# Four-tap convolution in a Mamba input stage: one tap and the bias made by ScalarE from the projection's PSUM bank

## The reference, cut to what matters

```
xz = layernorm(hidden) @ in_proj_w              # 256 -> 1024
x, z = split(xz, 2)                             # 512 and 512 channels
xpad = pad(x, 3 zeros ahead of each sequence)
acc = sum over k in 0..3 of conv_w[:, k] * xpad[:, k:k + seqlen, :]
x = silu(acc + conv_b)
x_dbl = x @ x_proj_w                            # 64 for dt, 16 for B, 16 for C
dt = softplus(dt_low @ dt_proj_w + dt_bias)
u = dt * x                                      # "du"; silu(z) is used later on
```

## Time and profile before

| | |
|---|---|
| runs | 2545.29, 2545.34, 2553.23 us (median 2545.34) |
| profiled execution | 2548.63 us, span 2546.9 us |
| TensorE busy | 2258.4 us (89%) |
| VectorE busy | 1786.6 us (70%) |
| ScalarE busy | 1339.8 us (53%) |
| GpSimd busy | 1340.4 us (53%) |
| mean granted clock of TensorE | 0.948 of full |
| the stage | from 0 to some 230 us |

### The profile page before, as it was taken

One profiled execution on the slowest core, in us unless ns is written; L12 is line 12 of the kernel. 1 busy time (PEld: TensorE's weight loads), 2 busy tenths in 40 slices (PEclk: granted clock), 3 DMA queues, 4 the chain that ended last, 5 costly groups with the idle time before them and its releaser, 6 DMA issues. The chain is left out here.

```text
span 2546.9 us, 34973 instructions
## 1 busy us (share of the span) xinstructions
PE 2258.4 (89%) x11358; PEld 1329.1 (52%) x11359; DVE 1786.6 (70%) x2734; ACT 1339.8 (53%) x2581; POOL 1340.4 (53%) x1024
## 2 busy tenths in 40 slices
PE   8895888989988988599986699999998569999998
PEld 3342444544544545599973334444444336666666
DVE  6998999999999997655557899999993651111100
ACT  5777887787788786322224456666665311111110
POOL 1545999899899895377755312222222123334332
PEclk9997999999999999799997789999998779999999
DMA  5457245125125112644437612222200503333322
GB/s 165 150 186 260 102 131 194 37 77 185 42 77 180 50 50 85 190 71 72 72 60 165 144 33 34 34 42 42 34 3 4 199 25 83 66 71 70 74 50 25
DMA packets 149681, 231.36 MB, mean 91 GB/s; under 512 B 26257, under 2 KB 98769, under 8 KB 149394
## 3 DMA queue, kind: packets, MB, share of 16 engines
q1 hardware_dynamic: 120258, 190.44, 24.8%
q0 software_dynamic: 29280, 39.11, 9.5%
HBM read 152.43 MB, written 81.66 MB: 92 GB/s over the span
## 5 line engine op out<-in xcount | busy, mean ns | idle before, releaser
L1263 POOL TENSOR_TENSOR scan_hC<-scan_h,scan_c_all 128x1024 f32<-128x1024 f32 x256 | 612.5, 2416 | 65.0 <-DVE scan_h L1118 63.8
L1118 DVE TENSOR_TENSOR_SCAN scan_h<-scan_dA,banks 128x1024 f32<-128x1024 f32 x224 | 504.5, 2275 | 21.3 <-ACT scan_dA L1040 12.9
L893 PE MATMUL banks<-scan_hC,all_ident 128*128 128x512 f32 x1024 | 486.9, 600 | 26.4 <-DVE scan_xc L1125 26.4
L2346 ACT ACTIVATE attn_pt<-banks 128x1024 f32<-128x1024 f32 (+3 forms) x384 | 292.3, 810 | 183.1 <-PE banks L2293 180.2
L1033 ACT ACTIVATE scan_scaled<-mamba_duT,mamba_bT 128x128 f32<-128x128 f32 x1024 | 312.0, 388 | 20.5 <-PE banks L870 20.1
L2230 POOL TENSOR_SCALAR_AFFINE_SELECT attn_pt<-attn_pt 128x256 f32<-128x256 f32 x256 | 102.6, 407 | 376.7 <-ACT attn_pt L2346 375.0
L893 PEld LDWEIGHTS banks<-scan_hC,all_ident 128*128 128x128 f32 x1024 | 185.3, 191 | 179.3 <-issue 129.2
L3084 DVE TENSOR_TENSOR ffn_y<-banks,ffn_gates 128x512 f32<-128x512 f32 x32 | 22.1, 691 | 334.7 <-PE banks L2842 328.0
L3131 POOL DMA_INDIRECT out<-ffn_y,ffn_ids x64 | 105.3, 1645 | 270.5 <-DVE ffn_y L3084 260.8
L2368 DVE TENSOR_REDUCE attn_m_lo<-banks 128x1 f32<-128x512 f32 (+3 forms) x368 | 225.9, 657 | 26.3 <-PE banks L2249 20.0
L2249 PE MATMUL banks<-attn_K,attn_Q 96*128 96x512 bf16 (+3 forms) x768 | 230.9, 340 | 7.1 <-DVE attn_mask L2358 5.9
(11 more groups left out here) (354 smaller groups left out, 3873.5 us busy)
## 6 DMA issues: line engine op xcount, KB each, us to landing
scan_c_all<-scratch_bc SPq DMA_DIRECT2D x64, 512.0 KB, 5.8
ffn_w<-in_e_w SPq DMA_DIRECT2D x16, 1024.0 KB, 5.4
attn_Q<-scratch_q SPq DMA_DIRECT2D x96, 128.0 KB, 4.1
scratch_x<-front_xc SPq DMA_DIRECT2D x8, 1024.0 KB, 5.8
scratch_z<-front_zs SPq DMA_DIRECT2D x8, 1024.0 KB, 7.5
scan_xc<-scratch_x SPq DMA_DIRECT2D x16, 512.0 KB, 3.6
scan_zs<-scratch_z SPq DMA_DIRECT2D x16, 512.0 KB, 4.6
scratch_dt<-front_lw SPq DMA_DIRECT2D x7, 1024.0 KB, 4.1
```

The source lines that it names most:

```text
L893: mm = pe.matmul(PS[:, YB + i, :], ident[:, :], hC[:, u % NHC, i * BANK:(i + 1) * BANK], start=s == 0, stop=s == NST - 1, skip_group_check ...
L1118: dve.tensor_tensor_scan(h[:, u % NH, :], decay, drive, 0.0, ALU.mult, ALU.add).then_inc(scanned, 1)
L1263: pool.tensor_tensor(hC[:, u % NHC, :], h[:, u % NH, :], c_all[:, s, :], ALU.mult).then_inc(hC_done, 1)
L2346: act.activation(pt[:, at % 4, 2 * pair:2 * pair + 2, 0:width], PS[:, ST + 2 * pair:ST + 2 * pair + 2, 0:width], ACT.Exp, scale=HD ** -0.5 ...
```

## The change

ScalarE now does two things with each bank of x: first it makes `conv = taps[3] * bank + cbias` (an Identity activation with scale and bias read per partition), counted by a new semaphore `own_tap`; then it copies the bank into `xpad` as before. VectorE makes three operations where it made four: tap 0 is added to `conv` into the accumulator bank, tap 1 to the accumulator, tap 2 to the accumulator into `conv`. ScalarE waits for the weights' loads before its first step, and the wait for the SiLU of the chunk before, which frees `conv`, moves from VectorE to ScalarE.

```
+        DTAPS = NTAP - 1
+        own_tap = n.sem("own_tap")
 def copy_x(q, m):
     act.wait_ge(in_psum, 2 * MT * q + m + 1)
     h = q % HB
     if q >= HB:
-        act.wait_ge(conv_step, NTAP * (MT * (q - 1 if h == 0 else q - HB) + m + 1))
+        act.wait_ge(conv_step, DTAPS * (MT * (q - 1 if h == 0 else q - HB) + m + 1))
+    if q:
+        act.wait_ge(silu_x, MT * (q - 1) + m + 1)
+    act.activation(conv[:, m, :], PS[:, bank_of("x", q, m), :], ACT.Identity, scale=taps[:, m, DTAPS:NTAP],
+                   bias=cbias[:, m:m + 1]).then_inc(own_tap, 1)
     act.activation(xpad[:, m, NTAP - 1 + h * CH:NTAP - 1 + (h + 1) * CH], PS[:, bank_of("x", q, m), :],
                    ACT.Copy).then_inc(x_copied, 1)
 def silu_conv(q, m):
-    act.wait_ge(conv_step, NTAP * (MT * q + m + 1))
+    act.wait_ge(conv_step, DTAPS * (MT * q + m + 1))
...
 act.wait_ge(made, 4)
+loads.wait(act)
...
 def convolve(q, m):
     h = q % HB
     acc = PS[:, CBANK, :]
-    for tap in range(NTAP):
+    for tap in range(DTAPS):
         src = xpad[:, m, h * CH + tap:h * CH + tap + CH]
         if tap == 0:
+            dve.wait_ge(own_tap, MT * q + m + 1)
             dve.wait_ge(x_copied, MT * q + m + 1)
-            if q or m:
-                dve.wait_ge(conv_step, NTAP * (MT * q + m))
-            dve.tensor_scalar(acc, src, taps[:, m, 0:1], cbias[:, m:m + 1],
-                              ALU.mult, ALU.add).then_inc(conv_step, 1)
-        else:
-            dve.wait_ge(conv_step, NTAP * (MT * q + m) + tap)
-            if tap == NTAP - 1 and q:
-                dve.wait_ge(silu_x, MT * (q - 1) + m + 1)
-            dve.scalar_tensor_tensor(out=conv[:, m, :] if tap == NTAP - 1 else acc, in0=src,
-                                     scalar=taps[:, m, tap:tap + 1], in1=acc, op0=ALU.mult,
-                                     op1=ALU.add).then_inc(conv_step, 1)
+        if q or m or tap:
+            dve.wait_ge(conv_step, DTAPS * (MT * q + m) + tap)
+        dve.scalar_tensor_tensor(out=conv[:, m, :] if tap == DTAPS - 1 else acc, in0=src,
+                                 scalar=taps[:, m, tap:tap + 1], in1=conv[:, m, :] if tap == 0 else acc,
+                                 op0=ALU.mult, op1=ALU.add).then_inc(conv_step, 1)
```

## The result

The changed kernel takes 2553.05 us (median of 22 runs, 2550.76 to 2556.26). The kernel before takes 2548.38 (median of 22 runs, 2545.29 to 2553.23), 3.0 above the median of the three runs that the prediction started from. The medians are 4.7 us apart. The ratio of the runs is 1.0016, 95% interval 1.0009 to 1.0022: 4.1 us slower (2.3 to 5.6). That lies within the 0.3% that were called no change, but it is not zero, and the time is 1 us over the range.

What follows compares the result with a forecast made beforehand. VectorE and TensorE were taken as nearly tied, VectorE holding TensorE through ScalarE's copies. Terms + 0.7 + 0.7 + 1.3 - 0.8 - 1.8 gave + 0.1 us, so 2545.5 from a median of 2545.34; range 2540 to 2552.

Steps and rivals of the forecast that it cites:

- rival (b): Identity makes ScalarE load tables ahead of x_proj, 2 x 1.28 us a step: + 18, 2563 us; chance 0.04.
- step 0: First step: the tap ahead of the copy of x(0,3) makes TensorE 0.7 us later.
- the stall of dt(1): TensorE's wait for VectorE's `less` before chunk 1's dt projection, 5.86 us before, stays, near 6.5 us.
- Steady steps: From one x_proj to the next: 22.32 us for 22.53, a gain of 0.8 us over four steps.
- rival (a): VectorE's relief reaches the stage's end, TensorE runs without stalls: - 13.6, 2531.8 us; chance 0.08 in full.
- weak form: Rival (a) with the standard deviation half as late and taps near 0.6 us: - 5, 2540 us; chance 0.08.
- signs of being wrong: A `less` stall under 3 us, steps of 21.8, or the stage's last VectorE instruction moved over 4 us.
- the price of tap 0 within its bounds: VectorE's new tap 0, two SBUF inputs, result in PSUM: 756 ns taken, bounds 0.62 and 0.81 us.
- the tail: Stage's end: less VectorE backlog before the last SiLU turns + 2.0 us into + 0.15, a gain of 1.8.
- The stall of 0.55 us a step: TensorE, ready at 133.84, waits before x_proj for ScalarE's copy of x(5,1), behind its tap, until about 134.40.
- rival (c): Slightly slower: ScalarE taps of 1.0 us and a longer lower clock behind the stall: + 4 to + 6, 2550 us; chance 0.10.

Runs made afterwards that it cites:

- e7: Changed kernel with GpSimd's products dt and du cut to 8 of 512 columns: 2551.97 us, ratio 1.0012.
- e12: Changed kernel, but tap 0's second input is the accumulator bank in PSUM, not conv in SBUF: 2549.34 us, ratio 1.0006.
- e13: e12 with ScalarE's square root of the next group moved right behind the copy of x(q,0): 2540.72 us, ratio 0.9972.
- e2: Kernel before with VectorE's tap 3 left out and no new work on ScalarE: 2542.05 us, ratio 0.9976.
- e6: Changed kernel with the square root early and ScalarE's taps made from xpad behind the copies: 2542.71 us, ratio 0.9982.
- e9: Kernel before with the change for groups 2 and 3 alone, taps from xpad behind all copies, and the square root early: 2537.44 us, ratio 0.9965.
- e10: Kernel before with the change for groups 2 and 3 alone, taps from xpad behind all copies, square root not moved: 2549.69 us, ratio 1.0008.
- e5: Kernel before with only ScalarE's square root moved right behind the copy of x(q,0): 2541.08 us, ratio 0.9973.
- e8: Kernel before with GpSimd's products dt and du cut to 8 of 512 columns: 2544.79 us, ratio 0.9987.

## Why the prediction was wrong

**The median it started from**: of the 7.5 us between 2545.5 and 2553.05, 3.0 are the kernel before, whose 22 runs lie that much over the first three. 4.7 are the change, of which 0.1 was forecast. The range was missed by 1 us, and each of two errors is larger than that: this median, and the operand below.

**What was right.** The length of ScalarE's tap (0.77 forecast, 0.780), and that there are no further table loads (rival (b)). By the Trainium skill, "ScalarE: Activation LUTs", What ACT_TABLE_LOAD costs, the estimate was 0.80. TensorE 0.7 us late in step 0, once the later start is taken off; the square root of group 2 behind the taps; the stall of dt(1) at 6.34 us for "near 6.5". The square root's end lets VectorE's reciprocal begin, 66.44 for 65.26, and 0.7 of that is the start of the stage:

```profile
66.44 0.25 DVE L483 RECIPROCAL front_rstd<-front_rstd 128x16 f32<-128x16 f32 x1 [8.70 <-ACT front_rstd L347]
```

Steady steps of 22.32 were forecast; with all four of ScalarE's taps ahead of the copies they are 22.45 wherever VectorE is out of the way (e7, e12, e13). A dt(1) waiting over 3 us rules out rival (a), and e2 shows what its relief alone is worth: 6.1 us, the size of its weak form. Of the signs of being wrong one came: the stage's last VectorE instruction begins at 232.85 for 228.64, 4.2 us later.

**The step that failed: "VectorE's work in a step falls from 21.6 us ... to 18.3, so it has slack, and the price of tap 0 within its bounds costs nothing."** The price was outside the bounds: 0.985 us in the mean, up to 1.72 beside GpSimd. All the rows that bounded it have only one of their input tensors in SBUF. The Trainium skill, "GPSIMD Engine Reference", Key points, says that GpSimd shares its SBUF interfaces with VectorE and contends with its instructions that have two SBUF inputs: the rule that spoke against this change, and I hadn't weighed it. The traces agree: 0.985 us beside GpSimd at work, 0.761 with it quiet (e7), 0.753 with one input in PSUM (e12). The slack went into stretched operations, tap 0 and more still the short ones, whose price the sum of 18.3 had left as it was. So VectorE stayed 19.35 us busy of 20, where 17 were forecast, and with the long tap 0 it was late for the last SiLU of step 5. The operand's place is worth 2.1 us of the stage by e12 against the changed kernel: some 0.5 by x_proj(1) and dt(1) (GpSimd's rows come later too, and the transposes wait 1.65 us for them, 1.17 in e12 and 0.49 before), 0.2 of slow clock, 1.1 by the stall of 1.81 us, 0.3 in the tail. In the tail VectorE's softplus begins at 204.79, behind the split of B and C, though its Exp had ended at 204.0:

```profile
200.54 1.63 DVE L530 TENSOR_TENSOR front_bc_rest<-front_xd,mamba_bc_parts 32x512 f32<-32x512 f32 x1
202.21 1.38 DVE L532 CAST front_bc_mid<-front_bc_rest 32x512 bf16<-32x512 f32 x1
203.62 0.42 DVE L533 CAST mamba_bc_parts<-front_bc_rest 32x512 bf16<-32x512 f32 x1
...
204.79 1.23 DVE L512 TENSOR_SCALAR front_w<-front_u 128x2048 f32<-128x2048 f32 x1
```

**The stall of 0.55 us a step**, mis-sized: 0.68 measured, since x_proj starts 0.14 us after the copy's end and not 0.04. With a slow clock behind dt(1) that lasts a little longer (6.61 us for 6.10), and the rest of the tail, this is 1.3 us of the stage. It is what remains of rival (c), whose taps of 1.0 us did not come.

**The start**: 0.7 us of the 4.1 that the stage missed its forecast by (0.7 + 2.1 + 1.3) lie ahead of the first tap. Bank x(0,1) was read at 18.62 before and 19.32 after:

```profile
19.32 0.78 ACT L360 ACTIVATE front_conv<-banks,mamba_cbias,mamba_taps 128x512 f32<-128x512 f32 x1 [1.06 <-PE banks L284]
```

TensorE's instructions up to there are the same in both. The kernels with ScalarE's tap in this place read it between 18.36 and 20.03, those without any ScalarE tap between 18.41 and 18.79, and those with the tap elsewhere (e6, e9, e10) at 19.93, 19.48 and 18.65. Whether a part of it belongs to the change stays open.

**What the change could give.** With the square root and the operand out of the way (e13) the change is level with its counterpart (e5). So with the taps ahead of the copies nothing was to be gained even with tap 0 at the 0.75 us that I took. Taps behind the copies with a cheap tap 0 were not run, and what they would give stays open. By e12 the time would have been 2549.34 with that tap 0, in the range.

## What to carry to other kernels

An operation moved off an engine can change the ones that stay: count where each remaining operand lies, and what GpSimd does at that time, before you call the engine relieved. Taking work from the busiest engine pays only up to the next loop, so work out that engine's step first; here it was 22.45 us for 22.53. And look for the one instruction that stands behind others in a queue: moving a square root ahead of Exp and three copies was worth more than any division of the taps tried here.

## What the runs showed of the hardware

- A slowed engine doesn't show as idle, and relief of it need not show as idle time either (19.17 of 20 us in e12). Tap 0 takes 0.74 to 0.76 us alone, often 1.20 beside GpSimd and at most 1.72. VectorE's short casts stretch far more in proportion, 0.41 to 1.38 us for 32x512, and GpSimd's product `du` from 1316 to 1466 ns:

```profile
123.50 0.76 DVE L502 SCALAR_TENSOR_TENSOR banks<-front_xpad,mamba_taps,front_conv 128x512 f32<-128x512 f32 x1
...
125.97 1.20 DVE L502 SCALAR_TENSOR_TENSOR banks<-front_xpad,mamba_taps,front_conv 128x512 f32<-128x512 f32 x1
...
147.69 1.72 DVE L502 SCALAR_TENSOR_TENSOR banks<-front_xpad,mamba_taps,front_conv 128x512 f32<-128x512 f32 x1
```
```profile
L611 POOL TENSOR_TENSOR front_du<-front_lw,front_xc 128x512 f32<-128x512 f32 x28 | 40.2, 1466 | 0.0
```

- An operation with two of its input tensors in SBUF is no dearer than one with an input in PSUM as long as GpSimd is quiet (761 and 753 ns).
- TensorE's stall can cost twice. Behind 6.34 us of idle time eight matmuls took 6.61 us for 3.60 (granted clock 0.50 in the first 3 us of them, the lower of its two levels), and behind 4.63 us 5.37 for 3.60. The length of the wait before them doesn't settle it: behind the same 3.09 us x_proj(7) took 5.31 us in e5 and 3.67 in e8.
